# Order of clearing transfers, order of two VectorE steps, and extra TensorE products ahead of three stages of a fused MoE, attention and MoE kernel

## What is computed

```python
def _L0_ffn_ref(x, w_router, w_gate, w_up, w_down):
    logits = xt @ w_router
    probs = jax.nn.softmax(logits, axis=-1)
    top1 = jnp.argmax(probs, axis=-1)
    pos = jnp.cumsum(onehot, axis=0)[jnp.arange(T), top1] - 1
    accepted = pos < C
    slot = jnp.where(accepted, top1 * C + pos, E * C)
    buf = jnp.zeros((E * C + 1, H), dtype=x.dtype).at[slot].set(xt)
    g = jnp.einsum('ech,ehf->ecf', buf, w_gate)
    u = jnp.einsum('ech,ehf->ecf', buf, w_up)
    y = jnp.einsum('ecf,efh->ech', jax.nn.silu(g) * u, w_down)
    out_tok = jnp.where(accepted[:, None], out_tok * gate[:, None], 0.0)
    return (xt + out_tok).reshape(B, S, H)

x = x + 0.5 * _L0_ffn_ref(_layernorm(x), w_router, w_gate, w_up, w_down)
x = x + _L0_attn_ref(_layernorm(x), W_proj, A, Bp, D, W_delta, b_delta)
x = x + 0.5 * _L0_ffn_ref(_layernorm(x), w_router, w_gate, w_up, w_down)
```

## Time and profile before

| | |
|---|---|
| median of three runs | 1561.3 us (1559.84 to 1561.47) |
| the profiled execution | 1561.85 us, of which the recorded span is 1560.0 us |
| busy: PE, PEld, DVE, ACT, POOL | 1301.6, 1232.9, 1250.8, 1098.8, 678.0 us |
| mean granted TensorE clock | 0.925 of full speed |
| stages by the trace | route to about 230, experts to 636, attention to 1150, experts to the end |

### The profile page before, as it was taken

The page is one execution under the profiler, slowest core; times in us unless marked ns, Lnnn a source line. Parts: engine busy times, 40 slices in busy tenths (PEclk is TensorE's granted clock), DMA queues, the critical chain, the costliest instruction groups (busy, mean ns, idle before and its releaser), DMA issues. The chain is left out here.

```text
span 1560.0 us, 31181 instructions
## 1 busy us (share of the span) xinstructions
PE 1301.6 (83%) x10179; PEld 1232.9 (79%) x10179; DVE 1250.8 (80%) x3385; ACT 1098.8 (70%) x2343; POOL 678.0 (43%) x778
## 2 busy tenths in 40 slices
PE   5545209999999999599999999987539999999996
PEld 4323108999999999599888889887439999999996
DVE  8959807999999999288999999999837777777775
ACT  6756307777777776489888889886647777777773
POOL 0566762443444334312245644544633444334443
PEclk9776558999999999799999999998859999999999
DMA  9995346666677662731111222111244444444440
GB/s 326 402 378 184 138 149 223 223 231 211 210 228 226 222 211 79 241 110 42 41 47 49 87 91 80 60 59 53 65 140 133 119 131 136 137 141 124 146 126 24
DMA packets 149775, 234.72 MB, mean 150 GB/s; under 512 B 24333, under 2 KB 124390, under 8 KB 147568
## 3 DMA queue, kind: packets, MB, share of 16 engines
q1 hardware_dynamic: 121968, 188.24, 37.2%
q0 software_dynamic: 27648, 44.50, 8.3%
HBM read 128.51 MB, written 136.48 MB: 170 GB/s over the span
## 5 line engine op out<-in xcount | busy, mean ns | idle before, releaser
L1027 PE MATMUL ps<-xs,ws 128*128 128x320 f32 x3072 | 465.1, 311 | 2.0 <-issue 2.0
L1027 PEld LDWEIGHTS ps<-xs,ws 128*128 128x128 f32 x3072 | 455.4, 189 | 2.8 <-issue 2.8
L1027 PE MATMUL ps<-ws,hs 128*128 128x256 f32 x1920 | 261.8, 288 | 10.8 <-DVE x L958 7.1
L851 POOL DMA_INDIRECT slots_and_rows<-x x160 | 164.6, 1028 | 243.2 <-DVE x L968 203.5
L851 POOL DMA_INDIRECT out<-x x160 | 157.8, 987 | 247.8 <-DVE x L958 166.7
L1027 PEld LDWEIGHTS ps<-ws,hs 128*128 128x128 f32 x1920 | 238.9, 190 | 24.0 <-issue 22.3
L890 ACT ACTIVATE x<-x 128x256 f32<-128x256 f32 x320 | 165.0, 594 | 58.2 <-DMA x<-slots_and_rows 43.7
L979 DVE TENSOR_TENSOR hf<-ps,sg 128x320 f32<-128x320 f32 x256 | 125.2, 489 | 88.3 <-ACT sg L911 87.7
L872 ACT CAST xs<-ps 128x512 fp32r<-128x512 f32 (+1 forms) x192 | 98.3, 513 | 131.0 <-PE ps L1020 131.0
L373 POOL DMA_INDIRECT slots_and_rows<-x,slot x128 | 126.9, 991 | 98.3 <-issue 86.5
L373 POOL DMA_INDIRECT slots<-x,slot x128 | 132.4, 1035 | 79.7 <-issue 44.3
(11 more groups left out here) (137 smaller groups left out, 2318.1 us busy)
## 6 DMA issues: line engine op xcount, KB each, us to landing
slots<-blank SPq DMA_DIRECT2D x16, 1310.0 KB
slots_and_rows<-blank SPq DMA_DIRECT2D x32, 655.0 KB, 4.5
x<-slots_and_rows SPq DMA_DIRECT2D x31, 655.0 KB, 3.9
x<-slots SPq DMA_DIRECT2D x31, 655.0 KB, 4.3
x<-slots_and_rows SPq DMA_DIRECT2D x32, 516.0 KB, 8.7
x<-in_x SPq DMA_DIRECT2D x32, 512.0 KB, 9.4
wraw<-in_w_gate SPq DMA_DIRECT2D x64, 256.0 KB, 2.7
wraw<-in_w_up SPq DMA_DIRECT2D x64, 256.0 KB
```

The lines of the kernel that those rows point to most:

```text
L851: nc.gpsimd.indirect_dma_start(out=rows, out_offset=bass.IndirectOffsetOnAxis(ap=factor(e, k, F_ID).bitcast(U32), axis=0), in_=XG[:, e % G ...
L1027: ins = pe.matmul(dst, left(a, k), right(b, k), start=(n == 0), stop=(n == len(terms) - 1))
```

## The change

Three things are changed. SP issues six of the 16 clearing pieces where all stood, and the other ten behind the last eight quarters of x. DVE does `y_sum` of quad 0 ahead of `x_lo` of quad 1. PE gets a helper, `keep_busy`, whose products nobody reads: 10 ahead of the first transposes of either expert run, 16 ahead of the first gram product. Each is 128x512 in bf16. Ahead of them PE now waits until all scatters of the stage before have landed.

```diff
+        def keep_busy(pe, bank, times):
+
+            for k in range(times):
+                pe.matmul(ps[:, bank, :], ONES, FRESH[TB][:, 0:512], start=True, stop=True)
+
...
+                FILL_FIRST = 6
...
                     sp.wait_ge(blanked, 2)
-                    for n in range(NFILL):
+                    for n in range(FILL_FIRST):
                         fill2(sp, n)
                     for q in range(4 * XR, NQ4):
                         if q % 4 == 0:
                             sp.wait_ge(tail.scattered[q // 4 - XR], 16 * TB)
                         stream.load(sp, q)
+                    for n in range(FILL_FIRST, NFILL):
+                        fill2(sp, n)
...
                         if more:
                             x_lo(e + 1, 0)
                         if more:
+                            y_sum(e, 0)
                             x_lo(e + 1, 1)
-                        if more:
-                            y_sum(e, 0)
                             y_sum(e, 1)
...
+                    before.all_scattered(pe)
+                    keep_busy(pe, 7, 10)
                     turn_in(first, range(NQ))
...
                     pe.wait_ge(s_att, 80)
+                    for k in range(GR):
+                        pe.wait_ge(y_out[k], 16 * ET * len(range(k, E, GR)))
+                    keep_busy(pe, BZ[1], 16)
```

## The result

The changed kernel takes 1524.0 us (median of five runs, 1523.9 to 1528.4); the kernel before took 1561.5 beside it. The ratio is 0.9771, with a 95% interval from 0.9756 to 0.9785. The forecast was 1535.4 with a range from 1529 to 1545. The direction was right, and the gain was 11 us larger than forecast. The profiled run took 1527.6 us, its span 1525.8 against 1560.0 before, so the traces have 34.2 us to explain.

A forecast was written before the change was run, and what follows sets the result against it. POOL's scatters, stalled by late x loads, were taken to bound the route, and PE both expert runs. 1561.85 - 13.4 - 9.2 - 2.5 - 0.8 = 1535.95, less 0.55 for the median: 1535.4 us, range 1529 to 1545.

The forecast's parts named there:

- Part 1: Route: with ten clearing pieces moved behind the x loads, DVE's stall and POOL's 13.4 us stall go; -13.4 us.
- Part 2: Expert runs: `y_sum` of quad 0 earlier removes PE's wait of 0.152 us an expert, 62 times, less 0.2; -9.2 us.
- the bounds: Expert runs, order of the sums: gain between -4.7 us (one run alone) and -9.4 us.
- The rival of the first run's DVE: First expert run: DVE, nearly full with moments, becomes the bound and the 0.15 us wait returns; 1540.0 us, chance 0.12.
- The 0.2 us that I subtracted: First expert run: DVE also makes moments and has little room ahead of step m = 3; 0.2 us off the gain.
- Part 3: Attention's start: 16 unread products raise PE's clock, so gram runs fast and the first transpose comes earlier; -2.5 us.
- Part 4: Both expert starts: ten unread products speed some transposes, gate products begin at 1.2 GHz again; -0.4 us each, -0.8 together.
- One sign of being wrong: Expert and attention starts: PE's transposes starting later behind the unread products would show the prediction wrong; no size given.
- a held clock: Rival: clock held everywhere, attention -3.1 and experts -5.7 us in place of -3.3 together; 1529.9 us, chance 0.10.

The follow-up runs named there:

- chip 9: Follow-up set on one chip: kernel before 1561.5 us; changed kernel 1527.2; changed kernel with moments one step later and six more unread products in the gaps 1518.0.

## Why the forecast was right in direction and wrong in size

**Part 1, -13.4: measured -12.6.** Right. POOL's second stall is gone, the first stayed, DVE's wait is gone and the pitch held. The stall that went was 13.42 us less the ordinary 0.30 between two scatters, a correction the step lacked. That leaves 13.1. The other 0.5 us lie in the pace of the 80 scatters behind the stall, 1.286 us apart instead of 1.280. The last scatter came at 214.98, forecast "near 214".

**Part 2, -9.2: measured -18.6. This is the step that failed.** Its mechanism was right; the price of the wait for `y_sum`, 0.152 us an expert, was not: 0.387 went. The term was "0.152 us both times", made from PE's missing busy time (4.57 / 30) times 62. PE's busy time runs to a modelled end of each product. The two transposes have rows of 0.38 us, and the next product can start 0.13 us behind them when nothing holds it. So the first 0.25 us of the wait lay under their rows, by the traces: 0.54 from start to start before, less 0.13, is 0.41, against the idle column's 0.15. The trace of before had the right price in two places: the start-to-start time, and the weight loads, idle 0.36 us 31 times, 11.2 us in the second run. By that row the term would have been 62 x 0.36 = 22. The section on the profile before even says that a group's pitch is read from start to start; I did so for the products and not for the wait.

Nor did the bounds help. -9.4 as the far end came from the same reading, so the range left out what a second view would have put in. With the measured term in place of 9.2, and nothing else altered, the forecast would have been 1535.4 - 9.4 = 1526.0, against 1524.0. That it comes so near owes something to luck: the sum took the median 0.55 us below the profiled run, and it lay 3.6 below.

The Trainium skill ("Perfetto Trace Analysis", Tensor Engine Instruction) says that the end of a TensorE instruction is estimated and not observed, and under "Identifying the Most-Contended Engine" that matmul busy time is a poor measure and the busy share of the weight loads a better one. The trace agrees. In the bulk of the second run PE was short of its window by 4.57 us before, the weight loads by 10.97 (353.03 busy of 364), which is 0.37 an expert, and the measured gain was 0.387.

**The rival of the first run's DVE** was given 0.12, as "a wait for L979", with the whole 0.15 coming back. Its mechanism did occur, in the step named (m = 3, for L987 in the changed kernel), and took 0.17 of 0.39 us. The 0.2 us that I subtracted for it should have been 31 x 0.174 = 5.4 (0.387 less 0.213). Under the price of 0.152 it would have eaten the first run's whole gain. Under the real one it ate less than half.

**Part 3, -2.5: measured -2.8 at the first transpose, -2.3 over the stage.** Right, and so was its place (14.28 us behind the load, forecast 14). On chip 9 it was 2.7 (14.07 against 16.75).

**Part 4, -0.8: measured about -0.7 for both starts together, by luck.** The first start gave 1.4 (8.0 less the pitch's 6.6), the second lost 0.7 (11.3 less 12.0), where 0.4 was forecast for each. From SP's first load to the end of the 48 gate products it took:

| us | first start, before and changed | second start, before and changed |
|---|---|---|
| the compared traces | 19.00, 17.75 | 18.25, 19.03 |
| chip 9 | 18.43, 18.00 | 18.15, 18.82 |

The sum of the two is -0.5 in one pair and +0.2 in the other, so the ten products ahead of the experts brought nothing that can be told from none. The forecast was right in that the clock fell in the gaps. The second start lost both times: in the compared traces its first rows reached ACT 3.98 us behind SP's load, against 2.91 before; on chip 9 they came in time (2.93), but the gate products took 9.99 us against 8.79. One sign of being wrong showed at two of these four starts. The first transposes followed ACT's first row by 1.14 us before; behind the unread products it was 1.59 us at the first start (222.16 less 220.57), and 1.38 at the second on chip 9 (1131.62 less 1130.24).

**Still open.** Of five runs of the changed kernel three lie at 1523.9 to 1524.0 us and two at 1527.6 and 1528.4. Both traces of it are of the upper kind, so what the lower ones save isn't known, and with it the 3.2 us of the median gain beyond the traces. The clearing has no run by itself on an undisturbed chip, as said. And what stops ACT on the other chips is not known.

## What to carry to other kernels

Price a wait of TensorE by the time from start to start against the same place without the wait, or by the idle time of its weight loads. The idle column ahead of a matmul leaves out whatever lies under the modelled end of the one before. When two views of one wait differ by a factor of two, the range has to hold both. And products that only raise the clock gave a reliable gain at the expert starts only where they went on through the gaps until the dense work started; ahead of attention, where one gap of 1.30 us was left, they gave it without that.

## What the runs showed of the hardware

With ten unread products, then four transposes, 1.66 us of idling, six transposes and 1.02 us of idling, the granted clock went 1.00, 0.62, 0.50 in the three windows above. Six further products of 128x512 in those gaps held it at 1.00, at all four starts of the two kernels that have them (7.27 or 7.28 us for the 48 gate products; 9.29 and 9.99 without the six on chip 9). Without the six it held at one start of 13, so the fall is the rule here and not certain. The forecast had put a held clock at 0.10 and had not thought of filling the gaps.

The Trainium skill ("TensorE: Matmul & The Clock Gate", Part 4: PE-mode transpose) says that the full clock doesn't engage for transposes. The traces differ as to their speed once other products have raised the clock: four took 0.66 us at 221.51, in a window at 1.00, and 1.12 at 1154.34 before. Whether transposes alone raise it, no run here shows. Its other half, that they don't count as a busy PE in the same way, isn't contradicted: the clock fell while PE had only ten transposes and gaps.

The same program needed 1561, 1632 to 1634 or 1671 to 1675 us, each on other chips. The longer times lie in the route, the first expert run and attention, and not in the second expert run. The share of the DMA engines doesn't order them: in the trace of before it is 0.73 and 0.62 in the first two, but 0.25 in attention against 0.41 in the second expert run. In every trace of the longer kind ACT has 48.7 to 66.7 us of waits for L390 put down to "remote" in the route, and in none of the others any; what causes them isn't shown. A change whose gain lies in such a stage (the clearing: -12.6 us by the trace on one chip, 0.9997 on another) has to be timed on a chip without it.
